# Identity products in TensorE's gaps, flips between the scan's last links, and ScalarE in place of GpSimd for the scan's normalised rows

## What is computed

```python
x = x + mamba(layernorm(x))         # state-space layer: 256 channels, 16 states, scan over 512 steps
x = x + moe(layernorm(x))           # 8 experts 128 -> 512 -> 128; each token takes one expert
x = x + attention(layernorm(x))     # 8 heads, q and k of 64, bias by distance, softmax
x = x + moe(layernorm(x))           # the same experts again
# in mamba, for each state s:  h = dA_t * h + dBu_t ;  y_t = sum over s of h * C_t
```

## Time and profile before

| | us |
|---|---|
| median of 3 runs (lowest, highest) | 1245.97 (1245.11, 1248.42) |
| the profiled execution | 1244.75 |
| its span, first to last instruction | 1242.9 |
| busy: TensorE, VectorE, ScalarE, GpSimd | 1050.2, 907.7, 840.1, 540.3 |
| mean granted clock of TensorE | 0.942 of full speed |

### The profile page before, as it was taken

How to read it: one execution, slowest core, us unless ns; L and a number is a source line. 1 busy time by engine, 2 the same in 40 slices (tenths; PEclk the granted TensorE clock), 3 DMA queues, 4 the chain that set the end, 5 groups by cost and what they waited for, 6 DMA issues and landing times. The chain is left out here.

```text
span 1242.9 us, 24539 instructions
## 1 busy us (share of the span) xinstructions
PE 1050.2 (84%) x7470; PEld 755.6 (61%) x7470; DVE 907.7 (73%) x1967; ACT 840.1 (68%) x1736; POOL 540.3 (43%) x363
## 2 busy tenths in 40 slices
PE   2875499988888888769949999989999999992897
PEld 1442388888888888549934454545454555551897
DVE  7697789989889889546635686857685867673565
ACT  4897599988888889346625666747574757571564
POOL 0389588999999999524420001010101010011344
PEclk9898599999999999889978999999998999995899
DMA  3000244434674664133311000000000000001331
GB/s 91 4 2 4 88 114 132 126 120 124 195 209 125 179 191 123 53 93 98 111 43 35 1 2 18 1 19 1 18 0 19 1 18 9 10 18 56 96 92 47
DMA packets 84425, 83.40 MB, mean 67 GB/s; under 512 B 23735, under 2 KB 62396, under 8 KB 84320
## 3 DMA queue, kind: packets, MB, share of 16 engines
q1 hardware_dynamic: 75440, 60.20, 17.9%
q0 software_dynamic: 5568, 12.66, 2.9%
q10 hardware_dynamic: 3312, 9.33, 2.5%
HBM read 65.73 MB, written 17.35 MB: 67 GB/s over the span
## 5 line engine op out<-in xcount | busy, mean ns | idle before, releaser
L956 DVE TENSOR_TENSOR_SCAN h<-d_a,p_dbu 128x1024 f32<-128x1024 f32 x128 | 289.0, 2278 | 33.1 <-ACT d_a L735 24.0
L686 POOL TENSOR_TENSOR h<-h,c_rep 128x1024 f32<-128x1024 f32 x126 | 294.7, 2371 | 18.5 <-DVE h L956 16.5
L1896 ACT ACTIVATE arena<-arena,at_min 128x512 f32<-128x512 f32 x256 | 183.3, 720 | 120.5 <-DVE at_min L2007 118.2
L2007 DVE CUSTOM_DVE_ANT_0 arena<-at_p_scores,arena 128x512 f32<-128x512 f32 x256 | 174.5, 685 | 84.5 <-PE at_p_scores L1771 48.3
L1257 POOL TENSOR_SCALAR r_row<-r_row 128x4 f32<-128x4 f32 x16 | 3.7, 234 | 472.2 <-DVEq L1162 472.2
L735 ACT ACTIVATE d_a<-arena,a_exp 128x511 f32<-128x511 f32 x256 | 169.3, 710 | 16.5 <-DVE h L956 16.4
L1778 PEld LDWEIGHTS at_p_probs_T<-ident,arena 128*128 128x128 f32 x1024 | 113.1, 142 | 95.6 <-issue 69.5
L1771 PE MATMUL at_p_scores<-arena,at_q_T 64*128 64x512 f32 x512 | 162.2, 649 | 7.1 <-DVE at_min L2007 5.4
L727 ACT ACTIVATE b_du_T<-arena,b_T 128x256 f32<-128x256 f32 x392 | 166.0, 495 | 0.1
L1778 PE MATMUL at_p_probs_T<-ident,arena 128*128 128x128 f32 x1024 | 159.0, 284 | 4.0 <-ACT arena L1896 2.3
L856 PE MATMUL p_y_T<-ident,h 128*128 128x128 f32 x1024 | 133.5, 273 | 5.8 <-POOL h L686 5.7
(11 more groups left out here) (244 smaller groups left out, 1604.3 us busy)
## 6 DMA issues: line engine op xcount, KB each, us to landing
c_rep<-c_rows SPq DMA_DIRECT2D x128, 256.0 KB, 3.7
f_row<-expert_rows SPq DMA_DIRECT2D x78, 129.0 KB
diag_b<-diag_rows SPq DMA_DIRECT2D x30, 256.0 KB, 4.1
arena<-in_w_all ACTq DMA_DIRECT2D x8, 578.0 KB, 4.6
arena<-bias_by_distance ACTq DMA_DIRECT2D x8, 448.0 KB, 4.4
x_tok<-in_x SPq DMA_DIRECT2D x4, 512.0 KB, 4.9
x_tok<-x_between SPq DMA_DIRECT2D x8, 256.0 KB, 2.8
diag_rows<-diag_b SPq DMA_DIRECT2D x4, 256.0 KB, 5.2
```

The lines of the kernel that those rows point to most:

```text
L686: nc.gpsimd.tensor_tensor(h[:, n % HS, :, :], h[:, n % HS, :, :], cc, ALU.mult).then_inc(prod_done, 1)
L956: nc.vector.tensor_tensor_scan(h[:, n % HS, :, :].rearrange("p c t -> p (c t)"), da[:, s % 2, :, :].rearrange("p c t -> p (c t)"), p_dbu[: ...
L1896: nc.scalar.activation(pr[:, slot, :], sc[:, slot, :], ACT.Exp, scale=-1.0, bias=mn[:, slot:slot + 1]).then_inc(probs_ready, 1)
L2007: V.tensor_tensor_reduce(sc[:, slot, :], psc[:, s % SCB, :], band[:, hd, w0:w0 + T], 1.0, 3.0e38, ALU.add, ALU.min, mn[:, slot:slot + 1]). ...
```

## The change

- `keep_busy(bank, products)` issues products of the identity matrix with itself into a PSUM bank that nobody reads. There are 9 in setup near the end of the statistics, 7 at the start of the front, 7 and 2 at the start of each expert layer, 9 and four times 3 in attention's first head, and 3, 3, 3, 14 and 3 in its last tail.
- At the end of the scan the flips are spread between the last links on TensorE, VectorE takes the gate of the last batch before the last router stages of batch 6, and ScalarE takes eleven more flips before its padding DMAs.
- In the scan, the normalised rows are made by four activations on ScalarE after `exps(b, 11)`, with scale rstd and bias -mean*rstd; the bias is a new instruction on VectorE at step 9. GpSimd's `pool_rows` goes.

```diff
+    def keep_busy(self, bank, products):
+        for n in range(products):
+            self.nc.tensor.matmul(bank[:, 0:P], self.ident[:], self.ident[:], start=True, stop=True)
...
+        @block.tensor                      # setup
+        def _(pe):
+            pe.wait_ge(identity_made, 1)
+            pe.wait_ge(dve_step, MOMENTS - 3 * TPB)
+            k.keep_busy(p_idle, 9)
...
+            k.keep_busy(pdt[:, 0, :], 7)   # front, TensorE's first
             pe.wait_ge(w_loaded, 16 * 7)
...
-                    if s == 10 and b > 0:  # scan, GpSimd
-                        rt.pool_rows(pool, b - 1)
...
                     exps(b, s)             # scan, ScalarE
+                    if number > 0 and s == 11:
+                        rt.act_normed(act, b - 1)
...
             late(B - 2, 1)                 # scan's end, ScalarE
+            for n in range(0, 5):
+                at.take_flipped(act, n)
             rt.act_rows(act, B - 1)
-            at.take_flipped(act, 0)
             rt.act_rstd(act, B - 1)
-            for n in range(1, 4):
+            for n in range(5, 9):
                 at.take_flipped(act, n)
             rt.act_turned(act, B - 1)
-            for n in range(4, 6):
-                at.take_flipped(act, n)
+            at.take_flipped(act, 9)
             rt.act_exps(act, B - 1)
-            at.take_flipped(act, 6)
-            at.take_flipped(act, 7)
+            at.take_flipped(act, 10)
+            at.take_flipped(act, 11)
             plan.pad_ends(act, nc.scalar, range(5, E_N))
-            for n in range(8, 2 * H):
+            for n in range(12, 2 * H):
                 at.take_flipped(act, n)
...
             pe.wait_ge(scanned, B * NS)    # scan's end, TensorE
+            at.flip(pe, 0, 3)
             late(B - 2, 2)
-            for s in range(5, 8):
-                early(B - 1, s)
-            at.flip(pe, 0, 5)
+            early(B - 1, 5)
+            at.flip(pe, 3, 4)
+            early(B - 1, 6)
+            at.flip(pe, 4, 5)
+            early(B - 1, 7)
+            at.flip(pe, 5, 9)
             early(B - 1, 13)
-            at.flip(pe, 5, 6)
+            at.flip(pe, 9, 10)
             early(B - 1, 14)
-            at.flip(pe, 6, 7)
+            at.flip(pe, 10, 11)
             late(B - 1, 2)
-            at.flip(pe, 7, 2 * H)
+            at.flip(pe, 11, 2 * H)
...
-            EARLY = {0: 8, 1: 8, 4: 14, 5: 15}
+            EARLY = {0: 8, 1: 8, 3: 9, 4: 14, 5: 15}
...
-            for s in range(NS):            # scan's end, VectorE
+            early(B - 1, 2)
+            late(B - 2, 0)
+            late(B - 2, 1)
+            early(B - 1, 5)
+            late(B - 2, 2)
+            late(B - 2, 3)
+            early(B - 1, 6)
+            for s in range(4, NS):
                 late(B - 2, s)
-            for s in range(8):
-                early(B - 1, s)
-                if s == 6:
-                    plan.make_pad(dve)
+            plan.make_pad(dve)
+            early(B - 1, 7)
...
+        elif stage == 3 and self.in_psum:
+            dve.wait_ge(self.rstd_ready, 1 + b)
+            V.scalar_tensor_tensor(out=self.shift, in0=self.mv[:, :, 0], scalar=-1.0, in1=self.rstd,
+                                   op0=ALU.mult, op1=ALU.mult).then_inc(self.shift_ready, 1)
...
+    def act_normed(self, act, b):
+        act.wait_ge(self.shift_ready, 1 + b)
+        self.rows_out(act, b)
+        for j in range(TPB):
+            ins = self.k.nc.scalar.activation(self.row[:, j, 0:D], self.k.x[:, b * TPB + j, :], ACT.Identity,
+                                              scale=self.rstd[:, j:j + 1], bias=self.shift[:, j:j + 1])
+        ins.then_inc(self.ln_ready, 1)
...
+            k.keep_busy(p_idle, 7)         # both expert layers
             turn(0, 0)
+            k.keep_busy(p_idle, 2)
             turn(0, 1)
...
+            IDLE_BEFORE = {5: 3, 7: 3, 9: 3, 14: 14, 15: 3}
...
+            pe.wait_ge(x_there, 1)         # attention
+            k.keep_busy(pot, 9)
             for s in range(LATE):
+                if s in (19, 21, 23, 25):
+                    k.keep_busy(pot, 3)
                 head(-1, s)
...
             for s in range(ST):
+                if s in IDLE_BEFORE:
+                    k.keep_busy(psc[:, 0, :], IDLE_BEFORE[s])
                 tail(B, B % 2, s)
```

More of the change, by code:

```diff
@@ L202, in setup @@
         dve_step, args_ready, act_step, rr_ready = S("dve_step"), S("args_ready"), S("act_step"), S("rr_ready")
+        p_idle = k.ps("p_idle", [P, T], ctx=c)
+        MOMENTS = 2 * NT
         block = c.enter_context(nc.Block())
+        @block.tensor
[3 more added lines that the diff above has]
+            k.keep_busy(p_idle, 9)
         @block.sync
@@ L1059, in __init__ @@
             self.logit, self.eps = p_small[:, 0:n].rearrange("p (j e) -> p j e", j=TPB), sb("eps", [P, 1])
+            self.shift, self.shift_ready = self.veps, S("shift_ready")
             self.steps = 18
@@ L1242, in start_pool @@
         pool.sem_inc(self.rows_free, 1)
-    def pool_rows(self, pool, b):
-        pool.wait_ge(self.rstd_ready, 1 + b + self.rstd_from)
-        self.rows_out(pool, b)
-        for j in range(TPB):
-            ins = self.k.nc.gpsimd.tensor_scalar(self.row[:, j, 0:D], self.k.x[:, b * TPB + j, :], self.mv[:, j, 0:1],
-                                                 self.rstd[:, j:j + 1], ALU.subtract, ALU.mult)
-        ins.then_inc(self.ln_ready, 1)
     def pool_send(self, pool, b):
@@ L1367, in ffn @@
         py = k.ps(name + "_p_y", [P, YR, T], ctx=c)
+        p_idle = k.ps(name + "_p_idle", [P, T], ctx=c)
         S = lambda n: k.sem(f"{name}_experts_{n}", c)
```

## The result

The changed kernel takes 1263.25 us (median of 4 runs, 1262.48 to 1266.03) against 1245.54 in the same comparison: a ratio of 1.0146, with a 95% interval of 1.0124 to 1.0169. I had predicted 1231.5, faster, in a range of 1218 to 1242. It is slower by 1.5%, above that range. The profiled execution took 1263.58 us, 1.8 of it outside its span of 1261.8.

A forecast was written before the change was run, and what follows sets the result against it. GpSimd seemed to bind the scan by a little, with cold TensorE clocks costing at stage seams. Terms 5.3 + 2.3 + 1.9 + 2.1 + 0.9 + 2.1 - 0.2 gave 14.4 us gained, so 1231.5 us, range 1218 to 1242.

The forecast's parts named there:

- VectorE one small operation (0.1, the spacing of its neighbours): Scan: the added VectorE instruction for the normalised rows' bias would cost 0.1 us a batch.
- the bias from VectorE, which itself waits for ScalarE's rstd: Scan: possible cause of ScalarE idling before the normalised rows, listed as a sign of being wrong; no size given.
- +15 us of the upper bound: Scan: worst case for moving the rows to ScalarE, all of the 1.65 and the 0.6 us a batch exposed.
- The rival that GpSimd's load is all that counts: Scan: GpSimd is the bound, a batch falls by 3.1 to 43.6 us, total 1212.7; chance 0.10.
- ScalarE's rows exposed in every batch: Scan: seven times 1.65 us lost, no gain from GpSimd, total 1242.9 us; chance 0.12.
- a loss of 0.2: Whole scan: steady batches gain 0.5 us each, batch 1 loses 1.65, waits for landed sends cost 1.5.
- The landing: Scan: ScalarE's normalised rows wait for the last row send to land, taken as 0.25 us in each of six batches.
- my slower rival: Scan: `act_normed` waits for the landed send; with 2 us of wait a batch, total 1254.9 us; chance 0.05.
- 4.3 us after it started: Scan's end: the last row send landed then or later, beside more traffic; used to price waits in the scan.
- two more router stages: Scan's last links: these before the second `take_g`, with flips and ranks, give back 1.6 us; net gain 2.1.
- some 8.4: Attention's head: length in us of the chain from transposes to first bias if warm from the start, a gain of 6.2.
- The third rival: Joints between stages: lead-in products end before the clock rises, smaller gains, total 1237.5 us; chance 0.15.

The follow-up runs named there:

- the mended kernel: Changed kernel, but ScalarE writes rstd a second time into PSUM and VectorE's small operation reads that copy: 1237.05 us, ratio 0.9911.
- the later sends: Changed kernel with GpSimd's four row sends at its step 9 instead of 7, small operation still reading SBUF twice: 1263.95 us, ratio 1.0151.
- all three mended versions: Changed kernel with the small operation reading PSUM: alone 1237.05 us, with the last links in the old order 1229.73, with sends before the gate 1226.05.
- the third order: Changed kernel, small operation reading PSUM, batch 6's router stages and sends before the last gate, flips still between the links: 1226.05 us, ratio 0.9846.

## Why the prediction was wrong

**The step that failed** is the term "VectorE one small operation (0.1, the spacing of its neighbours)". It measured 5.3 to 6.2 us in each of six batches, 34.5 us in all with batch 1's 0.14; mended, the kernel is 27.4 us faster by the spans. The neighbours from whose spacing I priced it, the router's small operations, read at most one tensor from SBUF each; this one reads two. The kernel before does hold the price. In its front an instruction of VectorE with two inputs in SBUF runs once with GpSimd idle (at 51.6) and six times beside one of GpSimd's (line, form, count: ns lowest/median/highest, first and last start), and the timeline shows one of the six:

```profile
L487 DVE TENSOR_TENSOR delta_log1p<-delta_low,delta_e x7: 1215/3352/3367, 51.6 to 120.0; 128x1024 f32<-128x1024 f32 x7
```

```profile
119.88 2.34 POOL L566 TENSOR_TENSOR arena<-delta_log1p,delta_pos 128x1024 f32<-128x1024 f32 x1
...
119.95 3.35 DVE L487 TENSOR_TENSOR delta_log1p<-delta_low,delta_e 128x1024 f32<-128x1024 f32 x1 [4.88 <-POOL delta_low L578]
...
122.30 3.21 POOL L569 TENSOR_TENSOR arena<-arena 128x1024 f32<-128x1024 f32 x1
```

It takes 1.2 us alone and 3.35 in the median, as it ends 1.08 us after GpSimd's instruction (122.22). The next one of GpSimd takes 3.21 us here and 3.2 in all seven batches, where others of its form take 2.34, which fits its being held up in turn. So here VectorE did get in between two instructions of GpSimd; the second waits for a semaphore of the first and starts 0.08 us after its end, while the products of the scan follow each other without a gap. In the timeline of the kernel before, GpSimd is busy like that just where the new instruction was to stand:

```profile
444.08 7.03 POOL L686 TENSOR_TENSOR h<-h,c_rep 128x1024 f32<-128x1024 f32 x3
```

I priced the new instruction by its size, when the row that bears on it is the one with its kinds of operands. That the gap is what decides whether VectorE gets in fits the front and both places in the scan, but not the rows that GpSimd starts at 419.23 without one; what lets VectorE in there stays open. The Trainium skill, "SBUF — State Buffer", section "Who interferes with whom", says that a VectorE instruction with two SBUF inputs contends with a GpSimd instruction that reads SBUF, and that one with at most one SBUF input, outside the modes that take both ports, does not. The traces agree: 5.6 us with two and 0.13 with one, in the midst of products.

Nor was it a rival. I named "the bias from VectorE, which itself waits for ScalarE's rstd" as a sign of being wrong, which is the place (ScalarE's idle time of 4.2 us before the rows) but not the mechanism. The +15 us of the upper bound held only ScalarE's own work and the landing, so the range ended too low.

**The rest of that part was right in mechanism.** Batch 1, where GpSimd had no backlog and the operation took 0.14 us, lost 1.6 us (predicted 1.65). With one input in PSUM a steady batch takes 46.1 us (predicted 46.2), ScalarE is busy 42.6 (42.6) and GpSimd 41.2 (41.5). The rival that GpSimd's load is all that counts would have given 43.6, and is out. ScalarE's rows exposed in every batch is out too: it had the scan lose 11.6 us, and from the first gate to the last scan step the mended kernel gains 0.5. My sum had a loss of 0.2 there, close, but in part by luck: the landing came to 2.15 us once, not 0.25 in each of six, and the last batch gained more than a steady one (from the loop's last gate to the last scan step 35.1 us against 36.3).

**The landing** was my slower rival, with 0.05. In the changed kernel it doesn't bind in the scan, because the small operation delays ScalarE past it. The price "4.3 us after it started" was neither the usual one nor a bound. Up to 3.0 us after the last send's start is what the later sends show, so that ScalarE's arrival 3.7 us after it, is just safe. But in one batch, the fourth, all three mended versions wait, for 1.6 to 2.15 us, and the rows are there only 5.4 to 6.0 us after the last send's start. That batch is the only one in which a load of 578 KB is issued 4.6 us before that send; a load of 448 KB at the same place two batches later goes with no wait, and that the first one delays the rows is not shown.

**The scan's last links** failed as a second step. I gained 2.1 and gave back "two more router stages"; measured, +3.2. I counted the stages on VectorE, but not what they release: the sends of batch 6, and behind their landing `act_rows`, `act_rstd` and the normalised rows. In the kernel before this wait was hidden, as ScalarE waited for `add` longer than for the landing. The wait is the one that `rows_out` makes, and I had used it for the scan and not here. The parts on which the gain rested (gate 1.3 us earlier, projection 2.05 for 3.51) are all in the trace, and the third order shows what they are worth with the sends early: 27.5 us, 2.8 below before.

**The identity products** were right: 12.5 us predicted, 12.4 measured alone. That the total fits so well is partly luck, as the parts miss both ways. Attention's head gained 4.6 for 5.3. The terms of its chain add up to 8.9 us, not to the "some 8.4" that I wrote, so by my own terms it gains 5.7 warm from the start, and 4.8 with the 0.95 that I took off. That 0.95 was not lost, as the four transposes took 0.72 us already; but from the two projections to the first bias it takes 4.7 us where I had 3.7, for the last projection and the first scores are two links of 1.0 and 1.3 us, and I gave both together 1.4. The tail gained 2.2 for 2.3, the second expert layer 1.8 for 2.1, the first 1.1 for 1.9, and 0.6 came in attention's loop, where I had nothing. The front gained 2.1 (its second transposes start 2.09 us earlier), above my bound of 1.7: I had 1.25 us for the first projection, and it gained 1.57 (3.55 to 1.98 us). In the expert layers the clock came up with the first hidden product, as predicted. The third rival, products that end before the clock rises, is out, and with it what I had drawn from the rule on transposes in the Trainium skill, "TensorE: Matmul & The Clock Gate", PE-mode transpose: in the version without the threes only the four transposes and a rest of 0.78 us lie between the nine products and the first projection of attention's head, and it took 1.10 us, warm. The trace of the kernel before could have told me more: at the scan's start, from 157.4 to 171.7 us, TensorE makes nothing but transposes (`spread`, `sum_up` and the turns of the next batch, one record each). Ten microseconds of it, columns as in the earlier trace rows:

```profile
160.00:170.00 10.00, 9.78 (x80) 1.00 0.40 96
```

Transposes alone kept the clock at 1.00 there, so the rule does not hold for them in this kernel; whether they alone raise it no run shows.

**The sum again, with the measured terms:** 1244.75 - 12.7 at the joints + 3.2 in the last links + 28.4 in the scan = 1263.65, against the profiled 1263.58. As these terms are read from the same two traces, this shows only that none is missing.

## What to carry to other kernels

Price an added instruction by the row that has its engine, its operands' memories and its neighbours on the other engines, before its size: four elements per partition cost 26 us here, more than all that the change won. Here a VectorE instruction with both tensors in SBUF, put where GpSimd worked through a backlog of products, waited for all of them and held up the scans that would have refilled it; moving one input to PSUM gained 27 us, and moving the DMAs beside the instruction nothing. Where links are reordered, follow each delayed instruction to the DMA that it starts and to whoever waits for its landing.

## What was not expected of the hardware

- A 128x4 VectorE instruction with both inputs in SBUF ran until GpSimd had no product left: 5.6 us over three products, 8.75 over four. It did not get in between two products that followed each other without a gap; in the front of the kernel before, where 0.08 us lay between two instructions of GpSimd, VectorE did get in. With one input in PSUM it took 0.13 us, beside indirect DMAs of GpSimd 0.14.
- The wait shows as busy time of VectorE, 47.8 us of a batch of 51.2, with no idle time ahead of it: only the mean of the group, 4933 ns for 128x4, gives it away.
- In attention's head rests of 0.78 us between projections left the granted clock at 1.00 (640.8 to 649.6 us of the version without the threes) behind nine products and four transposes, while the same rests in the kernel before went with a clock of 0.50; here the clock's level depended on what came before, not on the rests alone.
